# A two-layer transformer block on one core: new instruction order, score masks on GpSimd, three buffers of exponentials, paired products

## The chip, the cores and the metric

The kernel runs on one core of a Trainium2 chip. The metric is device microseconds from launch to end, the median of several runs. The core has five engines with a queue each: TensorE (PE, matmuls), VectorE (DVE), ScalarE (ACT), GpSimd (POOL) and SyncE (SP), which here only issues DMAs. Each queue runs in order, and queues meet only at semaphores. POOL can't read PSUM, where PE writes.

## The reference, cut to what matters

Eight sequences (batches) of 512 tokens with 256 features pass through two layers. Sixteen heads have 16 features each, T = 512, D = 256.

```python
# layer 0 (causal)
xm = layernorm(x) * (1 + sc_a) + sh_a
q, k, v = split(xm @ Wqkv)
scores = where(causal, q @ k.T * hd ** -0.5, -inf)
x = x + gt_a * ((softmax(scores) @ v) @ Wproj + bproj)
xm = layernorm(x) * (1 + sc_m) + sh_m
x = x + gt_m * (gelu(xm @ W1 + b1) @ W2 + b2)
# layer 1 (no mask)
h = sln(x, w)                      # layernorm, then gamma(w) * . + beta(w)
out = (softmax(q @ k.T) / 16) @ v  # q, k, v of h
h1 = out @ Wp.T + bp + x
return sln(h1, w) + h1
```

Scores, exponentials and sums must be as accurate as float32.

## The kernel before, in words

Batches follow each other as in a pipeline. Everything that an engine does is cut into named pieces, and one written-out list of names sets the order for all engines at once: each engine walks the list and does its own part of each name (`run_passes`, `one_pass`). Pass i of the list RING works on layer 0 of batch i, on layer 1 of batch i-1 and on the close of batch i-2. There are passes -1 to 9. Pass -1 has a list of its own (FIRST), and in passes 0, 8 and 9 the same RING is walked and the names of batches that don't exist are skipped. The names:

- `s`, a scan: one matmul of bf16 cuts of q and k for one head and 128 queries (L808) into one of two banks SX; in layer 0 a second small matmul (L811) adds -3e38 above the diagonal. DVE reduces the bank to the negated row maxima MX (L625). 64 scans for each layer of a batch: in layer 0 they are 128, 256, 384 or 512 columns wide, in layer 1 always 512.
- `nm..` and `max..`: POOL cuts the maxima of eight heads into three bf16 parts (L440 to L446), PE transposes them (L924), ACT copies them (L551) and issues a DMA that puts them as three more rows beside q (L553). The two halves of a layer are `a` and `b`.
- `a` and `p`: one step of attention, for four heads and 128 keys. PE makes four transposed score tiles (L795), three at `a` and one at `p`, and in layer 0 adds the mask CAUSAL_T to each with a second matmul (L798). ACT takes the exponentials into E (L502), which has two buffers. At `p` PE also forms the product of the step before with V (`pv`, L783), four heads side by side in 32 columns of the array each, in float32, so that each head has two instructions. 16 steps for a layer of a batch. At each fourth step ACT copies the sum OP out to OE (L489).
- `pack`, `recip`, `scale`, `proj`: SP moves the row sums (L338) and outputs (L340) by DMA, DVE inverts the sums (L743), they go through DRAM and come back spread out (L346, L351), DVE scales (L746), PE projects (L865) and DVE adds and takes statistics (L724 to L637). POOL takes the power -0.5 (L420).
- `q`, `k`, `v`, `turn`, `up_n`, `down_n`: the dense matmuls (L890, L865, L878, L911) through two banks DN. `stackq`, `stackk`: six DMAs each that put the three bf16 cuts of q or k into QS or KS (L386).
- `norm_o` and `close1`: the last norm. DVE writes (x - mean) * rstd into OUT (L672), POOL multiplies by gamma (L465), adds beta to the residual (L467) and adds both (L470), and SP stores (L374).

ACT fills the buffer of E for step n only when the product of step n-2 is done:

```python
wait(act, pv_done, at["step"].at(1, -1))          # L500
```

## Time and profile before

| | us |
|---|---|
| median of 3 runs (lowest to highest) | 1468.91 (1466.01 to 1469.76) |
| the profiled execution's own time | 1477.51 |
| its span, first to last instruction | 1475.7 |
| busy: PE, DVE, ACT, POOL | 1288.3, 866.4, 676.6, 230.4 |
| TensorE clock granted, mean | 0.925 of full speed |

The busy time of PE counts each matmul until its modelled end, and ends overlap with the next start. What a matmul takes from the stream is the distance from its start to the next start. A slice of the profile page is a fortieth of the span, 36.9 us, and its digits are tenths.

### The profile page before, as it was taken

Reading aid. Unit: us, or ns where it says so; the run is one execution under the profiler, and the core shown is the slowest. Engines: PE = TensorE matmul, PEld = TensorE weight load, DVE = VectorE, ACT = ScalarE, POOL = GpSimd, SP = SyncE. Lnnn points to the kernel's source line nnn. Section 1 sums busy time; section 2 is a strip of 40 time slices with the busy share of each in tenths; the row PEclk is TensorE's granted clock in tenths of the full one; section 3 lists DMA queues with packets and bytes.
Section 4 is the critical chain, followed back from the end, with each engine's and each line's share of the span. In section 5 each row is a group of like instructions: output and inputs, shape, how many; then the busy total and the mean of one; then the engine's idle time right before and its main releaser. Section 6 shows DMA issues by size and latency. Waiting matters only on the chain.

```text
span 1475.7 us, 19136 instructions
## 1 busy us (share of the span) xinstructions
PE 1288.3 (87%) x7052; PEld 614.3 (42%) x7052; DVE 866.4 (59%) x1739; ACT 676.6 (46%) x1328; POOL 230.4 (16%) x256
## 2 busy tenths in 40 slices
PE   6795979999889998999899989999899988995871
PEld 5343534444434543454444544354444542442211
DVE  2633367755876468746875487747775576425611
ACT  1061116465446445545556544545546545650360
POOL 3003000210112002300222003200221020202002
PEclk8597979999989999999999999999999999996685
DMA  6305030411514041501532061503341142014002
GB/s 171 113 16 130 1 84 18 106 27 16 124 32 114 2 104 51 131 1 21 134 78 55 4 136 28 118 2 70 84 103 30 16 117 53 2 16 122 1 1 52
DMA packets 57924, 91.61 MB, mean 62 GB/s; under 512 B 10622, under 2 KB 21470, under 8 KB 57830
## 3 DMA queue, kind: packets, MB, share of 16 engines
q1 hardware_dynamic: 56822, 89.57, 26.3%
q8 instruction: 56, 0.92, 0.3%
q10 hardware_dynamic: 1008, 0.81, 0.2%
q14 instruction: 38, 0.31, 0.1%
HBM read 25.46 MB, written 4.77 MB: 20 GB/s over the span
## 4 chain that ended last, share of the span: by engine, by line
PE 62%; DVE 17%; issue 6%; DMA 5%; ACT 4%; SPq 3%; POOL 1%; ACTq 0%; POOLq 0%; DVEq 0%
PE SX L808 11%; PE OP L783 11%; PE DN L865 10%; PE SC L795 10%; DVE MX L625 8%; PE DN L911 7%; PE DN L890 7%; DMA KS<-PART 2%; DMA OC<-OE 2%; DVE STAT L632 2%; ACT E L502 2%; SPq L386 2%; PE SX L811 2%; PE DN L878 1%; PE SC L798 1%
## 5 line engine op out<-in xcount | busy, mean ns | idle before, releaser
L625 DVE TENSOR_REDUCE MX<-SX 128x1 f32<-128x512 f32 (+3 forms) x1024 | 557.5, 585 | 297.4 <-PE SX L811 192.3
L502 ACT ACTIVATE E<-SC 128x512 f32<-128x512 f32 (+3 forms) x1024 | 469.6, 521 | 384.3 <-PE SC L795 194.1
L808 PE MATMUL SX<-KS,QS 96*128 96x512 bf16 (+3 forms) x1024 | 334.3, 370 | 81.9 <-DVE MX L625 70.4
L795 PE MATMUL SC<-QS,KS 99*128 99x512 bf16 (+3 forms) x1024 | 302.8, 356 | 20.1 <-ACT E L502 9.6
L783 PE MATMUL OP<-E,V 128*32 128x512 f32 (+3 forms) x2048 | 241.3, 544 | 1.1 <-ACT E L502 1.1
L795 PEld LDWEIGHTS SC<-QS,KS 99*128 99x128 bf16 x1024 | 98.7, 100 | 295.0 <-ACT E L502 181.4
L808 PEld LDWEIGHTS SX<-KS,QS 96*128 96x128 bf16 x1024 | 101.0, 101 | 228.3 <-DVE MX L625 159.9
L911 PE MATMUL DN<-XT,W 128*128 128x512 f32 x256 | 123.0, 606 | 2.7 <-ACT HID L544 1.8
L890 PE MATMUL DN<-XT,WQKV 128*128 128x512 f32 x256 | 119.4, 610 | 2.4 <-DVE X L686 1.3
L420 POOL TENSOR_TENSOR RSTD<-VE,HALF 128x4 f32<-128x4 f32 x32 | 32.5, 1017 | 545.5 <-DVE VE L637 545.5
L865 PE MATMUL DN<-W,HID 128*128 128x256 f32 x512 | 117.2, 382 | 0.0
L811 PE MATMUL SX<-CAUSAL,ID 128*128 128x128 bf16 x512 | 109.7, 233 | 0.0
L798 PE MATMUL SC<-CAUSAL_T,ID 128*128 128x128 bf16 x512 | 108.3, 227 | 0.0
L865 PEld LDWEIGHTS DN<-W,HID 128*128 128x128 f32 x512 | 95.1, 190 | 12.7
L865 PE MATMUL DN<-WP,OC 128*128 128x256 f32 x256 | 65.9, 415 | 34.0 <-DVE OC L746 23.9
L890 PEld LDWEIGHTS DN<-XT,WQKV 128*128 128x128 f32 x256 | 48.4, 195 | 56.9 <-issue 47.7
L865 PEld LDWEIGHTS DN<-WP,OC 128*128 128x128 f32 x256 | 52.4, 210 | 46.5 <-DVE OC L746 26.3
L783 PEld LDWEIGHTS OP<-E,V 128*32 128x32 f32 x2048 | 41.2, 110 | 69.0 <-issue 41.8
L724 DVE TENSOR_TENSOR TMP<-DN,ROW 128x512 f32<-128x512 f32 x32 | 22.0, 689 | 79.3 <-PE DN L865 77.5
L551 ACT ACTIVATE NT<-DN 24x512 bf16<-24x512 bf16 x32 | 18.8, 586 | 108.7 <-PE DN L924 102.0
L544 ACT ACTIVATE HID<-DN,VF 128x512 f32<-128x512 f32 x64 | 44.0, 687 | 51.2 <-PE DN L911 50.7
L525 ACT ACTIVATE XT<-DN,FM 128x512 f32<-128x512 f32 x48 | 35.2, 783 | 68.2 <-PE DN L878 68.2
(89 smaller groups left out, 984.2 us busy)
## 6 DMA issues: line engine op xcount, KB each, us to landing
QS<-PART SPq DMA_DIRECT2D x96, 256.0 KB, 5.3
KS<-PART SPq DMA_DIRECT2D x96, 256.0 KB, 7.6
OC<-OE SPq DMA_DIRECT2D x64, 128.0 KB
RB<-recip_sums SPq DMA_DIRECT2D x64, 128.0 KB, 2.6
XIN<-in_x SPq DMA_DIRECT2D x8, 512.0 KB, 9.5
ROW<-row_vectors SPq DMA_DIRECT2D x8, 512.0 KB, 3.8
out<-OUT SPq DMA_DIRECT2D x8, 512.0 KB, 2.9
W<-in_w SPq DMA_DIRECT2D x2, 1024.0 KB, 7.2
```

Of the source, the lines that this page charges most:

```text
L502: a.activation(E[:, at["step"].index() % 2, j, lo:T], SC[(4 * s + j) % 3][:, lo:T], ACT.Exp, scale=HD ** -0.5 if attend == 0 else 1.0)\
L525: a.activation(XT[:, ft, :], bank(ft)[:], ACT.Identity, scale=FM[:, first * KT + ft, bass.ds(b, 1)], bias=FM[:, (first + 1) * KT + ft, bas ...
L544: a.activation(HID[:, ht, :], bank(0)[:], ACT.Gelu, bias=B1[:, ht:ht + 1])\
L625: v.reduce_max(MX[:, qt, h:h + 1], SX[at["scan"].index() % 2][:, 0:w], AX.X, negate=True)\
L783: ins = t_.matmul(OP[32 * j:32 * j + 32, lo:T], V[attend][:, kt, h * VW:h * VW + 32], E[:, (at["step"].index() - 1) % 2, j, lo:T], start=k ...
L795: ins = t_.matmul(SC[u % 3][:, lo:T], KS[attend][0:ALL_ROWS, h, kt * P:kt * P + P], QS[attend][0:ALL_ROWS, h, lo:T], start=True, stop=atte ...
L798: ins = t_.matmul(SC[u % 3][:, lo:lo + P], ID16[:], CAUSAL_T[:], start=False, stop=True)
L808: ins = t_.matmul(bank[:, 0:w], QS[layer][0:CUT_ROWS, h, qt * P:qt * P + P], KS[layer][0:CUT_ROWS, h, 0:w], start=True, stop=layer == 1)
L811: ins = t_.matmul(bank[:, qt * P:w], ID16[:], CAUSAL[:], start=False, stop=True)
L865: ins = t_.matmul(psum[:, t % 2 * D:t % 2 * D + D], rows[:, kt, t * P:t * P + P], weights(kt), start=kt == 0, stop=kt == depth - 1)
L890: ins = t_.matmul(psum[:], WQKV[n][:, kt, lo:lo + P], XT[:, kt, :], start=kt == 0, stop=kt == KT - 1)
L911: ins = t_.matmul(psum[:], W1[:, kt, ht * P:ht * P + P], XT[:, kt, :], start=kt == 0, stop=kt == KT - 1)
```

## The change

The 11 passes are now written as three lists without skipped names: HEAD (passes -1, 0 and 1 together), RING (each of the passes 2 to 6) and TAIL (passes 7, 8 and 9 together). RING has 128 `s`, 32 `a`, 32 `p`, 16 `o` and 8 `t`; HEAD has 233 `s` and 48 steps, TAIL 151 `s` and 48 steps.

- The mask matmul of the scores (L798) is gone. POOL sets the entries of E above the diagonal to zero after the exponentials, one `affine_select` for each step of layer 0 over the 128 columns of four heads (128 in all). PE waits for it before the product.
- E has three buffers. The product is a name of its own, `o`, and does two steps at once (two times eight instructions). The copy of OP is `t`.
- For batch 0 of layer 0 and batch 7 of layer 1 the maxima go by four heads (`nm0_0`, `max0_0`, ...) and not by eight.
- `proj1`: POOL adds beta to the residual into RH. `gain1`: DVE forms (x - mean) * gamma, `close1`: DVE multiplies by rstd and adds RH. The three POOL operations go. The last batch is stored in two halves.
- The row sums have a semaphore of their own, so that the reciprocal doesn't wait for the four DMAs of the outputs; for the last batch ACT issues these four. `recip` and the loading of row vectors are parted (`row0`, `row1`). `keep0`'s copy on DVE goes: POOL reads XIN.
- The low cuts of q0 and k0 of batch 0 are made by DVE.

```diff
+HEAD = """
+    stat_a norm_a turn_a q0 mods stackq0 k0 stackk0 rows s s s s s s s s s s s s s s s s s s nm0_0 s s max0_0 s s
+    v0 s s s s s a row0 p s s s a s keep0 s p nm0_1 s s s s a s max0_1 s s s s p s s s s o s a s s s p a o s p a t
+    nm0_2 s s s p a max0_2 p s o a p s s a s s p stat_a a o p s s s norm_a t a s p a s o s nm0_3 turn_a p max0_3
+    q0 a p o a p a t p o a p o t pack0 k0 recip0 scale0 proj0 stackq0 v0 norm_m turn_m stackk0 s s up_0 s s up_1 s
+    s s s up_2 s s s s up_3 s s s s s s s s s up_4 s s up_5 s up_6 s s s s up_7 s s s s down_0 s s s s down_1 s s
+    nm0a max0a down_2 s s down_3 s a s row0 s s norm_1 keep0 p a s s turn_1 s s s s q1 p s stackq1 stat_a o s k1 s
...
 RING = """
+    row0 o s s a stackq1 p s s a stackk1 t s p s s s s s s o s s a pack1 s s p s a row1 s p s s s a s s p s s nm0b
+    s s recip1 o s s a s s p s s s max0b t s s s s a s scale1 p s a s o s s p a s o s p s a s p s t proj1 s a s p
+    a o p a s p s s s o keep0 gain1 s t a s p s a o nm1a close1 s p s stat_a a max1a s v1 p s a o norm_a s t p s
+    turn_a pack0 s a s s recip0 q0 s p s a o s stackq0 s p a scale0 s s p k0 a s s proj0 s s norm_m p v0 a o s p s
+    t turn_m a s s o p s s a s up_0 s p stackk0 s up_1 s up_2 s s nm1b o s s up_3 s hold1 s up_4 s s max1b s s
+    up_5 s s up_6 s s up_7 s s a s down_0 p s s a s down_1 s t p s down_2 s a s s p down_3 a o s p s a s p s s
+    norm_1 o s s t a s s turn_1 s nm0a s s p s max0a a s o p s s a s q1 s p k1""".split()
+TAIL = """
...
+    o p a p t q1 a o p a p k1 stackq1 stackk1 o s s s s t s s s s s s s s s s s s nm1_0 s s
+    s s max1_0 s s v1 s s a s s s p pack1 s a s s s p s nm1_1 a s o p s s a s s max1_1 p s s s s s recip1 o s s a
...
-        E = sb("E", [P, 2, 4, T])
+        E = sb("E", [P, 3, 4, T])
...
+                if kind == "attend":
+                    s, layer, half = what
+                    if half and layer == 0:
+                        lo = P * (s % TT)
+                        block = E[:, at["tick"].index() % 3, :, lo:lo + P]
+                        wait(pool, exp_done, at["head"].at(1, 4))
+                        g.affine_select(out=block, in_=block, compare_op=ALU.is_ge, fill=zero, base=0,
+                                        pattern=[[0, 4], [1, P]], channel_multiplier=-1)\
+                            .then_inc(masked_pool, 1)
...
-                            wait(act, pv_done, at["step"].at(1, -1))
+                            wait(act, pv_done, at["tick"].at(1, -2))
...
+            def product(at, layer, s, n):
+                wait(pe, exp_done, at["step"].at(4, 4 * n + 4))
+                if layer == 0:
+                    wait(pe, masked_pool, at["masked"].at(1, n + 1))
...
-                if attend == 0:
-                    ins = t_.matmul(SC[u % 3][:, lo:lo + P], ID16[:], CAUSAL_T[:], start=False, stop=True)
...
+                    if what == "proj1":
+                        wait(pool, row1_dma, at["rows1"].at(16))
+                        wait(pool, dense_done, at["dense"].at(1, 2))
+                        g.tensor_tensor(RH[:], TMP[:], ROW1[:, 1:2, :].to_broadcast([P, TT, D]), ALU.add)\
+                            .then_inc(plus_pool, 1)
...
+                elif what == "gain1":
+                        v.scalar_tensor_tensor(OUT[:, t, :], TMP[:, t, :], MV[:, t, 0:1], ROW1[:, 0, :],
+                                               ALU.subtract, ALU.mult).then_inc(gain_dve, 1)
+                elif what == "close1":
+                        v.scalar_tensor_tensor(OUT[:, t, :], OUT[:, t, :], RSTD[:, t:t + 1], RH[:, t, :],
+                                               ALU.mult, ALU.add).then_inc(norm_dve, 1)
```

## Rows read from the trace of the kernel before

**Rows 1.** Stretches: us; busy (count) of PE, PEld, DVE, ACT, POOL; clock; DMA; GB/s.
```profile
0.00:220.80 220.80, 166.35 (x816) 92.37 (x816) 96.10 (x222) 50.53 (x104) 28.50 (x42) 0.82 0.33 86
...
376.70:1189.00 812.30, 760.28 (x4363) 367.96 (x4362) 538.94 (x1076) 424.37 (x831) 140.82 (x150) 0.98 0.29 65
1189.00:1475.70 286.70, 213.61 (x1028) 83.30 (x1026) 130.77 (x245) 117.15 (x229) 40.99 (x38) 0.83 0.20 46
```
**Rows 2.** The same for the two parts of one middle pass.
```profile
540.40:620.00 79.60, 72.62 (x471) 33.76 (x469) 61.17 (x115) 41.04 (x96) 19.53 (x18) 0.98 0.48 112
620.00:701.30 81.30, 77.91 (x404) 39.69 (x404) 46.13 (x102) 43.70 (x72) 8.59 (x12) 1.00 0.11 21
```
**Rows 3.** Timeline of PE in a middle pass: start, us, instruction.
```profile
641.94 1.93 PE L911 MATMUL DN<-XT,W 128*128 128x512 f32 x4
643.71 0.38 PE L808 MATMUL SX<-KS,QS 96*128 96x512 bf16 x1
...
646.64 0.22 PE L811 MATMUL SX<-CAUSAL,ID 128*128 128x128 bf16 x1
646.79 1.07 PE L783 MATMUL OP<-E,V 128*32 128x512 f32 x8
647.79 0.39 PE L795 MATMUL SC<-QS,KS 99*128 99x512 bf16 x1
...
648.35 0.22 PE L811 MATMUL SX<-CAUSAL,ID 128*128 128x128 bf16 x1
648.41 0.43 PE L865 MATMUL DN<-W,HID 128*128 128x256 f32 x1
```
**Rows 4.** Groups by line on PE and POOL: count, busy, mean ns, idle before.
```profile
L798 PE MATMUL SC<-CAUSAL_T,ID 128*128 128x128 bf16 x512 | 108.3, 227 | 0.0
L403 POOL TENSOR_SCALAR_AFFINE_SELECT ID<-ID 128x128 f32<-128x128 f32 (+1 forms) x2 | 0.5, 292 | 0.2 <-POOL CAUSAL_T L400 0.2
```
**Rows 5.** Groups on DVE: one operation on two SBUF inputs, two lines.
```profile
L728 DVE TENSOR_TENSOR XR<-XR,TMP 128x512 f32<-128x512 f32 x16 | 18.6, 1165 | 0.5
L728 DVE TENSOR_TENSOR R<-XR,TMP 128x512 f32<-128x512 f32 x16 | 11.1, 692 | 0.5
```
**Rows 6.** Chain of waits at the start: start, us, what.
```profile
44.11 1.17 DVE MX L625 x2
...
70.68 2.76 DMA QS<-NT
...
119.56 4.51 DMA OC<-OE
...
148.18 3.61 PE DN L911 x4
```
**Rows 7.** Timeline: first score matmul of batch 1 on PE.
```profile
218.96 0.39 PE L795 MATMUL SC<-QS,KS 99*128 99x512 bf16 x1 [2.22 <-DMA QS<-NT]
```
**Rows 8.** Timeline near the end, DVE, SP, PE and POOL.
```profile
1330.69 1.23 DVE L695 TENSOR_TENSOR PART<-X,PART 128x1024 bf16<-128x1024 f32 x1
...
1337.02 4.51 SPq L386 DMA_DIRECT2D QS<-PART  x6
...
1353.26 1.03 PE L808 MATMUL SX<-KS,QS 96*128 96x512 bf16 x2 [8.39 <-DMA KS<-PART]
...
1377.18 0.22 POOL L440 TENSOR_SCALAR NMP<-MX 128x32 bf16<-128x32 f32 x1 [19.88 <-DVE MX L625]
...
1382.44 1.97 PE L795 MATMUL SC<-QS,KS 99*128 99x512 bf16 x4 [1.42 <-DMA QS<-NT]
```
**Rows 9.** Timeline of the last 36 us, the lines of the close.
```profile
1439.90 1.96 SPq L340 DMA_DIRECT2D OC<-OE  x2
1444.99 0.55 DVE L743 RECIPROCAL RR<-RS 128x64 f32<-128x64 f32 x1 [35.60 <-DMA OC<-OE]
...
1464.82 2.34 POOL L465 TENSOR_TENSOR OUT<-OUT,ROW 128x1024 f32<-128x1024 f32 x1 [1.50 <-DVE OUT L672]
...
1471.89 0.39 SPq L374 DMA_DIRECT2D out<-OUT  x1
```

More of the change, by code:

```diff
@@ L78 @@
 ADDS = {"proj0": {"dense": 2, "res": 2}, "proj1": {"dense": 2}, "down_0": {}, "down_2": {},
         "down_1": {"dense": 1, "res": 1}, "down_3": {"dense": 1, "res": 1},
-        "hold1": {"hold": 1}, "recip0": {"sums": 1, "rows0": 1, "bias": 1},
-        "recip1": {"sums": 1, "rows1": 1}, "pack0": {"pack": 1}, "pack1": {"pack": 1},
-        "scale0": {"scale": 1}, "scale1": {"scale": 1},
-        "keep0": {"keep": 1, "x_in": 1}, "close1": {"close": 1}, "stat_a": {},
+        "hold1": {"hold": 1}, "row0": {"rows0": 1, "bias": 1}, "row1": {"rows1": 1},
@@ L84 @@
+        "pack0": {"pack": 1}, "pack1": {"pack": 1}, "recip0": {"sums": 1}, "recip1": {"sums": 1}, "scale0": {"scale": 1}, "scale1": {"scale": 1},
+        "gain1": {"gain": 1}, "keep0": {"x_in": 1}, "close1": {"close": 1, "norm": 1}, "stat_a": {},
         "mods": {}, "rows": {}, "stackq0": {}, "stackq1": {}, "stackk0": {"stack0": 1}, "stackk1": {"stack1": 1}}
@@ L97 @@
 COUNTS = ("dense", "res", "bias", "maxima", "max0", "max1", "hold", "pack", "sums", "scale", "rows0",
[L98 to L99 removed]
+          "rows1", "x_in", "gain", "close", "stack0", "stack1", "high", "low", "norm", "head", "tick",
+          "step", "masked", "group", "scan", "halves")
 class Count:
@@ L122, in run_passes @@
     at["x_in"].n = 1
-    for i in range(-1, B + 2):
-        one_pass(at, work, i)
+    one_list(at, work, HEAD, (-1, 0, 1))
+    for i in range(2, B - 1):
+        one_list(at, work, RING, (i,))
+    one_list(at, work, TAIL, (B - 1, B, B + 1))
 def do_chunk(at, work, chunk, b):
@@ L155, in one_pass @@
+            work(at, "attend", (s, layer, 1), b)
+            at["head"].n += 4
+            at["tick"].n += 1
+        elif what == "o":
+            layer, b, s = products.pop(0)
+            products.pop(0)
+            work(at, "product", (s, layer), b)
+            at["step"].n += 2
+            at["masked"].n += 2 * (layer == 0)
+        elif what == "t":
+            layer, b, g = groups.pop(0)
+            work(at, "out", (g, layer), b)
+            at["group"].n += 1
         elif what == "s":
@@ L171, in two_layers @@
+            work(at, "scan", (layer, h, qt), b)
+            at["scan"].n += 1
+        else:
+            do_chunk(at, work, what, chunks[what].pop(0))
+    assert not steps and not products and not groups and not tiles
 def two_layers(nc, x, cond_t, wqkv0, wproj0, w1, w2, wada, wqkv1, wp1, wgb1, vecs, bv1, bp1, out):
@@ L545, in work @@
                         .then_inc(dense_done, 1)
-                elif what in ("max0a", "max0b", "max1a", "max1b"):
-                    n, first = int(what[3]), H // 2 * "ab".index(what[4])
+                elif what == "pack1" and b == B - 1:
+                    wait(act, out_act, at["group"].at())
+                    wait(act, scaled_dve, at["scale"].at())
+                    for j in range(4):
+                        act.dma_start(OC[64 * (j % 2):64 * (j % 2) + 64, j // 2, :],
+                                      OE[32 * j:32 * j + HD, :, :]).then_inc(compact_dma, 16)
+                elif what.startswith("max"):
+                    n, heads = int(what[3]), maxima_heads(what)
+                    rows = 3 * (heads.stop - heads.start)
                     psum = bank(0)
@@ L715, in work @@
                     wait(dve, bias_pool, at["bias"].at())
-                    if what == "proj0":
-                        wait(dve, close_pool, at["close"].at(3))
+                    wait(dve, plus_pool, at["gain"].at())
                     if what == "down_1":
@@ L832, in work @@
                     for j in range(3):
-                        score_t(at, attend, s, j)
+                        score_t(at, layer, s, j)
                     return
-                if kind == "last":
-                    pv(at, what, STEPS - 1)
+                if kind == "product":
+                    s, layer = what
+                    for n in range(2):
+                        product(at, layer, s + n, n)
+                    return
+                if kind != "chunk":
                     return
```

355 lines of the change are left out of this document (189 added, 166 removed), and 5 rows, old and new, of the table BEHIND.

## The prediction, made before the changed kernel ran

> **What bounds the kernel now.** I read the busy time by stretches first, then the order of starts on TensorE, then the chain at both ends. Cut where the attention of batches 2 and 7 begins, the span falls into a start, five full passes of 162.5 us (812.3 / 5) and an end [rows 1]. In the five passes PE is busy 94% at a clock of 0.98; no other engine passes 66%. At the start PE is busy 75% at a clock of 0.82, and in the last 286.7 us also 75% at 0.83. So there are three questions: what leaves PE's stream in the full passes, how much of the idle time at the ends can be filled, and what waits at the ends get shorter.
>
> A full pass has two unlike parts [rows 2]. In the first (scans of layer 1, attention of layer 0, the small dense pieces) PE is busy 72.6 of 79.6 us and DVE 61.2: PE does long dense pieces in which DVE, with only two banks of scans, runs dry, and then waits for DVE in turn. In the second (up, down, attention of layer 1) PE is busy 77.9 of 81.3 us and DVE only 46.1: PE alone is the bound there.
>
> Busy time overstates small matmuls. The masks of the scores stand with 108.3 us, 227 ns each [rows 4], but from a 128-column mask to the next start it is 0.06 us [rows 3]. That is the price that counts where PE is full.
>
> **The change part by part.** The sum is made against the profiled execution: 1477.5 us, 1.8 more than its span.
>
> *Masks of the scores.* 512 leave PE, 64 in each batch: 64 x 0.058 = 3.7 us a pass, all in the first part. In their place POOL has 16 selects of 512 elements a batch. The trace has selects of 128 elements at 0.29 us [rows 4] and POOL operations of 1024 elements with two inputs at 2.34 us [rows 9]. So one costs at least 0.29 and, by four times the small one or half the large one, at most 1.17 us; I take 1.0, nearest to both upper prices. 16 us beside the 19.5 us that POOL has in this part of 79.6 us [rows 2] is well covered. The new wait (product for mask) has queued behind it on PE all that follows. It is hidden because the pair of products comes later in the list than its exponentials, with `s` or an `a` between in nearly all cases, and ACT has a third buffer to write meanwhile. Without that cover each pair would cost 1.0 us: 8 pairs, 8 us a pass.
>
> *Paired products.* The start behind a mask is 0.15 us away when a product follows and 0.06 when a dense matmul does: 0.09 to get in. The two rounds of a product take 2 x 0.44 (four dense instructions of 512 columns take 1.77 us) = 0.89, but the next score comes after 1.00: 0.11 to get out [rows 3]. So a visit to the 32-column form costs 0.2 us besides its work. 16 visits fewer in a pass: 3.1 us, some 10 of 16 in the first part. No products stand back to back in these rows, so it is bounded: 0 to 3.1 us; I take nearly all.
>
> *What the five full passes get.* Up to 6.8 us leaves PE's stream. But 5.6 of it leaves the first part, where DVE keeps 61.2 busy us and its own idle moments behind the dense pieces. RING has the same number of scans ahead of `norm_m` as before (75), so the part's other limit doesn't move. I count the second part's 1.2 us whole and of the first part's 5.6 us two thirds: 5 us a pass, 25 us for five. Ends: 0 (the first part is as long as ever), and 6.8 plus the 7 us in which PE is idle there now, 13.8 a pass.
>
> *The DVE work* changes little: the copy of `keep0` goes, four passes over 256 columns come. It is not what ends a wait. Nothing for that.
>
> *The start.* (a) The first attention waits for 41 scans, which begin at 44.1 and end at 70.7: 0.65 us each [rows 6]. Now 18 scans do, so it begins some 15 us earlier. The end of that attention then hangs on the last of all 64 scans: 44 + 42 = 86, and v0, the maxima's chain and four steps put it near 110, where the copies out lie at 119.6 now: -9. (b) From there to the first up matmul are 28.6 us of waits in series [rows 6]; the sums no longer wait for the outputs' DMAs: -2. (c) From that matmul to the first scores of batch 1 are 70.8 us [rows 6, 7]: up, down, then scans, turn_1, q1 and k1, and only then the maxima. HEAD puts all 41 scans into up and down and the scores right behind down_3. That stretch needs 8 x 1.77 for up, 4 x 3.5 for down (the same columns twice) and 41 x 0.2 for scans = 36.5, some 2 more for waits: -32. (d) q1, k1 and turn_1 now stand under the attention of batch 1: +8 us of PE; with 87 scans in the same stretch DVE holds it up: +6. Pass 1 gets its own -5. Sum for the start: -34 us, ends -15 and -50.
>
> *The end.* (a) Pass 7: -5. (b) The last cuts of k1 are ready at 1331.9, but the DMAs of q and k stand in SP's queue behind `recip1` and start at 1337.0; those of k take from 1341.5 to 1353.3 until scans start. TAIL puts the stacks ahead of `pack1`, so k's can go at 1331.9: 9.6 us earlier at best; I take -8. (c) From the first scan to the last copies out are 86.6 us (1353.3 to 1439.9): 32 scans of 0.75, a chain of 5.3 until scores start, and 16 steps [rows 8, 9]. By groups of four heads the 64 scans run alongside the steps: 64 x 0.75 = 48, v1 and other pieces between them 5, chain 5.3, four steps of 2.5 (four exponentials of 512 columns), product and copy 2: 70. That is -16. (d) The close: the reciprocal comes 5.1 us after the last DMA's issue, -3 with sums apart and ACT issuing the outputs; three POOL operations from 1464.8 to the store at 1471.9 (7.1 us) turn into two halves of DVE work, of which one has to be done before the first store: -6 [rows 9]. In the new `proj1` POOL adds beta (2.34 us) ahead of the power, but the statistics on DVE cover it. Sum for the end: -38 us, ends -22 and -52.
>
> *Three buffers, the split of row0 and recip, DVE's cuts for batch 0:* nothing by themselves; they let the order above hold. SP has no wait that is new in kind, and `row0` stands at the head of RING, where its data has long been due when `proj0` comes. It does stand ahead of the first masks on POOL: where the row vectors land late, the masks are late too. I count this within the 5 us.
>
> **Sum.** -34 - 25 - 38 = -97: 1477.5 - 97 = 1380.5. The median of the runs stands at 1468.91 / 1477.51 = 0.994 of the profiled execution, so 1372 us.
>
> **A rule against the change.** One DVE operation with both inputs in SBUF takes 692 ns on average in one place and 1165 in another [rows 5]; the second place is where POOL works on large tiles. So a busier POOL can slow DVE. The Trainium skill (SBUF — State Buffer, section Who interferes with whom) says that a DVE instruction with two SBUF inputs and a GpSimd instruction that reads SBUF shut each other out for the whole of one of them, and that a reduction is never held up. By that rule, the trace agrees, and scans are safe while `gain1`, `close1`, `scale` and the residual adds are not.
>
> **The rivals.**
>
> 1. *The idle time of the first part is filled as well.* For: PE is no longer the fuller engine there, and DVE is at 61 of 79.6. Against: two banks, and the same dense pieces. 8.8 us more for each of seven passes: 1380.5 - 62 = 1319, or 1311 as a median; anything between counts here down from 1345.
> 2. *DVE sets the pace of the first part.* The passes stay at 162.5 us, and the start and end give only some -50: 1427, or 1419 as a median. For: 75 scans ahead of `norm_m` as before. Against: DVE isn't full in any stretch.
> 3. *Masks hold up DVE.* Some 11 operations with two SBUF inputs a pass, each waiting for one mask of 1.0 us: 11 x 8 = 88 us, 1460. For: the 1165 ns [rows 5]. Against: masks cover only a fifth of the part's time, and the three long POOL operations of `close1`, which did the same, go.
> 4. *POOL becomes the bound (slower).* If a select over four blocks takes far more than its element count says, the first part lasts 16 T + 19.5 us instead of 75. It eats the whole gain of 97 / 8 = 12 us a batch from T = 4.2 us on; at T = 4.5 it is 91.5, 17 us a batch more than forecast: 1372 + 135 = 1507. For: nothing in the trace shows this shape. Against: both nearest rows give under 1.2 us.
>
> **How the numbers follow.** Forecast 0.55 (its own range 1345 to 1395), rival 1 0.22, rival 2 0.13, rival 3 0.05, rival 4 0.05. The range 1315 to 1425 takes in rivals 1 and 2 but for their far ends, and is what the ends of the terms give: -50 - 69 - 52 leads to 1299, -15 - 0 - 22 to 1432. About 0.3%, 4 us, is what a measurement can tell from no change. Faster 0.93, same 0.02, slower 0.05 (rival 4).
>
> **What the changed profile would show.** No L798 group; 128 selects on POOL of about 1.0 us (over 4: rival 4). Sixteen product instructions in a row with 0.44 us from round to round across the pair. Full passes of 157 us; 149 speaks for rival 1, 162 for rival 2. First scores near 60 us, first up matmul near 137, scores of batch 1 near 176. At the end, scans of the last layer some 13 us earlier than 1353 less what went before, 70 us from there to the last copies, and no POOL operation behind the power. The DVE mean of residual adds and of `scale` shows rival 3. I am wrong if the full passes don't get shorter though PE's stream did, or if the ends, which carry 72 of the 97 us, wait for something that I don't see in the list, as DMAs queued behind each other on SP.

## The result and the profile after

The changed kernel takes 1389.97 us (median of 4 runs, 1387.18 to 1396.24) where the kernel before takes 1469.34 beside it (1466.01 to 1473.45): a ratio of 0.948, 95% interval 0.945 to 0.951. The forecast was 1372 with a range from 1315 to 1425. The direction held and the range held the time, but the forecast was 18 us too low, and its parts were further off than their sum. The profiled execution took 1391.76 us, 11.3 more than the sum of 1380.5. The rest of the 18 us is the step from a profiled execution to the median, 0.999 here and not 0.994: the one execution of the kernel before that was profiled is 8 us longer than its median, longer than each of its timed runs.

First the stretches, cut as in [rows 1] where the attention of batches 1, 2 and 7 begins. Columns: stretch; its us; busy (count) of PE, PEld, DVE, ACT, POOL; clock; DMA; GB/s. Busy time and clock are those of the changed kernel:

```profile
0.00:186.50 186.50, 135.62 (x703) 74.23 (x703) 81.97 (x193) 46.67 (x99) 32.88 (x59) 0.90 0.31 85
186.50:363.50 177.00, 161.21 (x818) 74.85 (x818) 109.26 (x219) 89.99 (x174) 34.45 (x44) 0.92 0.24 58
363.50:1127.90 764.40, 731.96 (x4040) 355.16 (x4039) 533.84 (x1091) 415.94 (x830) 173.23 (x220) 0.99 0.30 70
1127.90:1390.00 262.10, 207.13 (x999) 85.88 (x997) 141.68 (x267) 117.22 (x232) 37.85 (x55) 0.88 0.21 47
```

| | before | after | difference | forecast |
|---|---|---|---|---|
| start, to the attention of batch 2 | 376.7 | 363.5 | -13.2 | -34 |
| five full passes | 812.3 | 764.4 | -47.9 (-9.6 each) | -25 |
| from batch 7 to the end | 286.7 | 262.1 | -24.6 | -38 |

The five passes gave nearly twice what was forecast, the two ends half of it. Part of the first is the execution and not the kernel: the kernel of experiment 6, which has the median of the kernel before, was profiled at 1466.96 us, with 371.0, 802.9 and 291.2 us in the three stretches. Against it the passes gained 38.5 us and the ends 36.6. The RING of the changed kernel took 764.4 to 769.8 us in four profiles (changed, 7, 8 and 12), so a pass is known to about 1 us, in the kernel before to about 2. In the passes PE is busy 28.3 us less (760.28 to 731.96), 5.7 a pass, and idle 19.6 us less (52.0 to 32.4), 3.9 a pass. The forecast took 6.8 us a pass off PE's stream and let its idle time grow by 1.8.

Two products in a row on PE in a middle pass (start, us, instruction), to be laid beside [rows 3]:

```profile
598.78 1.92 PE L888 MATMUL OP<-E,V 128*32 128x512 f32 x16
600.64 0.39 PE L899 MATMUL SC<-QS,KS 99*128 99x512 bf16 x1
```

From the first of sixteen instructions to the score behind them are 1.86 us; two products apart took 2 x 1.00 [rows 3]. With one entry of 0.09 us saved as well, a pair is worth 0.23 us; the forecast had 0.2.

The groups that answer to [rows 4, 5] (line, form, count; busy, mean ns; idle before, and releaser):

```profile
L505 POOL TENSOR_SCALAR_AFFINE_SELECT E<-E 128x512 f32<-128x512 f32 x128 | 85.4, 669 | 338.6 <-ACT E L585 338.5
...
L833 DVE TENSOR_TENSOR XR<-XR,TMP 128x512 f32<-128x512 f32 x16 | 15.9, 992 | 0.5
```

A select takes 0.67 us, under the 1.0 that was taken, and of PE's waits only one, of 0.6 us, has the select as its releaser. The operation on XR became shorter (1165 to 992 ns) though POOL got busier; the same one into R stays at 692. The selects have no part in it: with the masks back on PE (experiment 1) it takes 990 ns. Nor do the three POOL operations of the old close stand beside it in the middle pass looked at: there the long one lies beside POOL's cut of 2.13 us and ends 0.54 us behind it, in both kernels. In the kernel before it begins 0.76 us after the cut,

```profile
614.61 2.13 POOL L433 TENSOR_TENSOR PART<-X,PART 128x1024 bf16<-128x1024 f32 x1
...
615.37 1.91 DVE L728 TENSOR_TENSOR XR<-XR,TMP 128x512 f32<-128x512 f32 x1
```

and in the changed one 1.02 us after it (588.18 behind 587.16), and so takes 1.65 us.

What lengthens it in other passes was not looked at. DVE's reductions of 512 columns take 685 ns in both kernels. Both facts agree with the rule quoted in the prediction (the Trainium skill, SBUF — State Buffer, section Who interferes with whom).

Where the wait at both ends is (timeline and chain; start, us, instruction), for [rows 6 to 9]:

```profile
63.83 0.81 PE L899 MATMUL SC<-QS,KS 99*128 99x512 bf16 x3
...
113.90 3.24 SPq L404 DMA_DIRECT2D OC<-OE  x4
...
140.48 1.95 PE L1014 MATMUL DN<-XT,W 128*128 128x512 f32 x4 [0.35 <-issue]
...
184.75 0.81 PE L899 MATMUL SC<-QS,KS 99*128 99x512 bf16 x3
...
1272.31 4.38 SPq L464 DMA_DIRECT2D KS<-PART  x6
...
1272.91 1.23 DVE L801 TENSOR_TENSOR PART<-X,PART 128x1024 bf16<-128x1024 f32 x1
...
1284.92 1.04 PE L909 MATMUL SX<-KS,QS 96*128 96x512 bf16 x2 [12.43 <-DMA KS<-PART]
...
1341.63 1.11 POOL L540 TENSOR_SCALAR NMP<-MX 128x16 bf16<-128x16 f32 x1 [13.95 <-DVE MX L723]
...
1361.79 3.58 ACTq L641 DMA_DIRECT2D OC<-OE  x4
```

The copies out are four DMAs at both ends, and the times here are those of the first one's issue. The prediction's rows have a later one of the four (119.56 and 1439.90); the same first issues in the kernel before are

```profile
117.61 3.25 SPq L340 DMA_DIRECT2D OC<-OE  x4
...
1438.61 3.25 SPq L340 DMA_DIRECT2D OC<-OE  x4
```

The reader is to see six distances: first scores at 63.8 (73.5 before), from the copies of the first attention to the first up matmul 26.6 us (30.6 before), from there to the scores of batch 1 44.3 (70.8 before), from the last cut of k to the scans that read it 10.8 (1274.14 to 1284.92; 21.3 before), from these scans to the last copies 76.9 (85.4 before), and from those to the end 28.2 (37.1 before).

### The profile page after: what moved, and what is told of

Read it like the earlier page. It is cut to its first block, busy times and chain, and to the rows that moved or that the text cites. A ratio compares the mean times of both kernels' runs of the same rounds, so it can differ in the third digit from the quotient of the medians.

```text
span 1390.0 us, 18485 instructions
## 1 busy us (share of the span) xinstructions
PE 1235.9 (89%) x6556; PEld 590.1 (42%) x6556; DVE 866.8 (62%) x1767; ACT 669.8 (48%) x1334; POOL 278.4 (20%) x378
## 4 chain that ended last, share of the span: by engine, by line
PE 67%; DVE 13%; ACT 5%; DMA 3%; issue 2%; SPq 2%; POOL 1%; ACTq 0%; DVEq 0%; POOLq 0%
PE DN L968 16%; PE OP L888 11%; PE SX L909 11%; PE SC L899 10%; DVE MX L723 10%; PE DN L1014 8%; PE DN L993 7%; ACT E L585 4%; PE DN L981 2%; PE SX L912 2%; DMA KS<-PART 1%; SPq L464 1%; DMA recip_sums<-RR 1%; DMA RB<-recip_sums 1%; DVE OUT L773 1%
## 5 line engine op out<-in xcount | busy, mean ns | idle before, releaser
L723 DVE TENSOR_REDUCE MX<-SX 128x1 f32<-128x512 f32 (+3 forms) x1024 | 557.1, 586 | 281.2 <-PE SX L912 176.0
L585 ACT ACTIVATE E<-SC 128x512 f32<-128x512 f32 (+3 forms) x1024 | 460.9, 523 | 380.9 <-PE SC L899 303.6
L909 PE MATMUL SX<-KS,QS 96*128 96x512 bf16 (+3 forms) x1024 | 344.0, 361 | 81.1 <-DVE MX L723 54.0
L899 PE MATMUL SC<-QS,KS 99*128 99x512 bf16 (+3 forms) x1024 | 281.2, 348 | 16.6 <-ACT E L585 9.6
L888 PE MATMUL OP<-E,V 128*32 128x512 f32 (+3 forms) x2048 | 215.2, 538 | 3.1 <-DVE X L793 1.4
L505 POOL TENSOR_SCALAR_AFFINE_SELECT E<-E 128x512 f32<-128x512 f32 x128 | 85.4, 669 | 338.6 <-ACT E L585 338.5
L993 PE MATMUL DN<-XT,WQKV 128*128 128x512 f32 x256 | 123.0, 626 | 0.9 <-ACT XT L616 0.9
L912 PE MATMUL SX<-CAUSAL,ID 128*128 128x128 bf16 x512 | 113.0, 227 | 0.0
L888 PEld LDWEIGHTS OP<-E,V 128*32 128x32 f32 x2048 | 54.9, 112 | 110.4 <-issue 83.2
L540 POOL TENSOR_SCALAR NMP<-MX 128x32 bf16<-128x32 f32 (+1 forms) x36 | 8.7, 241 | 278.5 <-DVE MX L723 232.0
L1014 PEld LDWEIGHTS DN<-XT,W 128*128 128x128 f32 x256 | 45.5, 191 | 43.2 <-issue 34.0
```

Of the source, the lines that this page charges most:

```text
L505: g.affine_select(out=block, in_=block, compare_op=ALU.is_ge, fill=zero, base=0, pattern=[[0, 4], [1, P]], channel_multiplier=-1)\
L585: a.activation(E[:, at["tick"].index() % 3, j, lo:T], SC[(at["head"].index() + j) % 3][:, lo:T], ACT.Exp, scale=HD ** -0.5 if layer == 0 e ...
L723: v.reduce_max(MX[:, qt, h:h + 1], SX[at["scan"].index() % 2][:, 0:w], AX.X, negate=True)\
L888: ins = t_.matmul(OP[32 * j:32 * j + 32, lo:T], V[layer][:, kt, h * VW:h * VW + 32], E[:, (at["step"].index() + n) % 3, j, lo:T], start=kt ...
L899: t_.matmul(SC[(at["head"].index() + j) % 3][:, lo:T], KS[layer][0:ALL_ROWS, h, kt * P:kt * P + P], QS[layer][0:ALL_ROWS, h, lo:T], start= ...
L909: ins = t_.matmul(bank[:, 0:w], QS[layer][0:CUT_ROWS, h, qt * P:qt * P + P], KS[layer][0:CUT_ROWS, h, 0:w], start=True, stop=layer == 1)
```

## The experiments

Each kernel was timed against the kernel before on the same chip, which took 1464 to 1467 us beside them. Ten of them start from the changed kernel (1390 us); of these 3 and 10 differ from it in the order of the middle passes alone, 5, 9 and 11 in the masks or pairs as well. 4 and 6 start from the kernel before. "Full passes" are the five stretches of the profiled execution, by five.

**1. Masks back on PE** (the changed kernel otherwise).

```diff
-                t_.matmul(SC[...][:, lo:T], KS[...], QS[...], start=True, stop=True).then_inc(head_full, 1)
+                ins = t_.matmul(SC[...][:, lo:T], KS[...], QS[...], start=True, stop=layer == 1)
+                if layer == 0:
+                    ins = t_.matmul(SC[...][:, lo:lo + P], ID16[:], CAUSAL_T[:], start=False, stop=True)
+                ins.then_inc(head_full, 1)
```

POOL's select and PE's wait for it are left out.

> The changed kernel, its order and the rest as they are, but the mask of the scores is again the second matmul on PE and POOL has no select. Theory A (PE's stream is what a full pass costs): 64 masks of 0.058 us come back in each of 8 batches, 3.7 us a pass, full passes 156.6 instead of 152.9 us, in all +30 us, 1420. Rival B (the new order made the passes shorter, and what left PE's stream in the first part is hidden behind DVE): +0 to +8 us, full passes 153 to 154.

Measured: 1391.17 us (ratio 0.949, 0.946 to 0.952), full passes of 153.3 us. Moving the masks is worth nothing that can be measured in this order. The forecast had counted it with 3.7 us of PE's stream a pass.

**2. No pairs.** The second product of a pair goes behind the next scan or score; where a dense piece comes next, the two stay together.

```diff
-                    for n in range(2):
-                        product(at, layer, s + n, n)
+                    product(at, layer, s, 0)
+                    late.append((kept, layer, s + 1, 1))   # issued behind the next s, a or p
```

> The changed kernel, but the second product of each pair is put behind the next scan or group of scores on PE (before a dense piece it stays behind the first). Theory A: a pair saves 0.2 us for one visit less to the 32-column form and, by the starts in the trace of after (409 instead of 433 ns from round to round inside a pair), some 0.1 more; 128 pairs x 0.33 = +42 us less those that stay paired, 1425 to 1432, full passes 157 to 158. Rival B: the passes have slack for it, +0 to +12 us.

Measured: 1417.07 us (0.967, 0.964 to 0.971), full passes of 157.1 us. Pairs are worth 4.2 us a pass, 27 us in all.

**3. The old order of the middle passes, first try.** RING has the names in the order of before, with all new mechanisms (pairs, three buffers, masks on POOL, the new close); the ends stay as changed.

> The changed kernel with RING in the order of the kernel before (products where they stood, now in twos at each second p; recip1, scale1 and close1 moved by a few names so that nothing waits in a new place); HEAD and TAIL as changed. Five full passes run in the old order with the new mechanisms. Theory A: masks 3.7 and pairs 5.3 us a pass are most of the 9.6 us that a full pass lost, so full passes take 153 to 155 us and the whole 1390 to 1402. Rival B: the order is most of it, full passes 158 to 161 us and the whole 1415 to 1430.

Measured: 1480.98 us (1.011, 1.007 to 1.014), passes of 169.9. Slower than the kernel before, though every part that was added is in it.

**4. Masks on POOL in the kernel before**, nothing else changed.

```diff
+                if kind == "attend" and half and layer == 0:
+                    wait(pool, exp_done, at["head"].at(1, 4))
+                    g.affine_select(out=block, in_=block, compare_op=ALU.is_ge, fill=zero, ...)
-                    ins = t_.matmul(SC[u % 3][:, lo:lo + P], ID16[:], CAUSAL_T[:], start=False, stop=True)
```

> The kernel before with one edit: the mask of the scores leaves PE and is a select on POOL, two buffers and single products as they were. Theory A: 3.7 us a batch, -30 us, 1440, if the select (0.67 us in the trace of after) is over when the product comes. Rival B: no gain, since the first part is held by DVE: 1465 to 1470. Rival C: without pairs and a third buffer PE stands behind the select, up to 0.7 us in 128 steps: 1470 to 1530.

Measured: 1564.79 us (1.068, 1.063 to 1.072), passes of 175.5. Over the five passes PE waits 21 times, 47.5 us in all, for a select that came last. The timelines of POOL and PE show the longest such place of one pass:

```profile
591.77 2.35 POOL L478 TENSOR_TENSOR OUT<-OUT,ROW 128x1024 f32<-128x1024 f32 x1
594.08 2.48 POOL L480 TENSOR_TENSOR TMP<-TMP,ROW 128x1024 f32<-128x1024 f32 x1
596.64 2.34 POOL L483 TENSOR_TENSOR OUT<-OUT,TMP 128x1024 f32<-128x1024 f32 x1
598.93 0.69 POOL L424 TENSOR_SCALAR_AFFINE_SELECT E<-E 128x512 f32<-128x512 f32 x1
```

```profile
599.76 0.87 PE L798 MATMUL OP<-E,V 128*32 128x384 f32 x4 [3.65 <-POOL E L424]
```

A select stands in POOL's queue behind the three operations of the old `close1`, and PE stands for 3.65 us. Three more stalls of this pass come when a select stands behind the power (0.39 and 2.35 us) or behind a cut (2.44 us). The clock follows. It has two levels, 1.0 (2.4 GHz) and 0.5 (1.2 GHz), and a stretch shows their mean: 0.91 over the five passes. Around two of these stalls, the one of 2.35 us before 585.48 and the one of 3.65 us before 599.76:

```profile
584.00:586.00 2.00, 0.52 (x8) 0.23 (x8) 0.83 (x2) 0.00 (x0) 1.33 (x2) 0.65 0.00 0
586.00:594.00 8.00, 8.00 (x39) 2.21 (x31) 4.52 (x8) 4.21 (x9) 3.46 (x3) 0.50 0.00 1
...
596.00:598.00 2.00, 0.11 (x1) 0.00 (x0) 2.00 (x2) 0.82 (x3) 1.92 (x2) 1.00 0.00 0
...
600.00:610.00 10.00, 9.90 (x45) 3.07 (x38) 6.07 (x10) 4.40 (x12) 1.91 (x3) 0.50 0.15 51
...
612.00:614.00 2.00, 2.00 (x15) 0.55 (x13) 1.29 (x2) 1.08 (x3) 0.00 (x0) 1.00 0.04 8
```

Behind the first stall PE works without a gap at 0.50 for 8 us, is back at 1.00 when the next stall begins, and works 10 us more at 0.50 behind that one: each stall is paid a second time.

**5. As 3, with masks on PE.**

> As e3_old_ring, but with the masks of the scores on PE as well: RING in the old order, products in twos, three buffers, new closing norm, no work of attention on POOL. So far: masks back on PE cost nothing (full passes 153.3), unpairing costs 4.2 us a pass, and the old order with all the new mechanisms takes 169.9 us a pass, more than the 162.5 of before. Theory C: the masks on POOL are what the old order can't bear (their select stands behind other work on POOL and bare before the product), and pairs give their 4 us there too: full passes 157 to 160 us, 1415 to 1430, and the rest of the way to 153 is the order. Rival D: my old order with new names has waits of its own (recip1, row vectors), whatever the masks do: full passes 167 to 171 us, 1470 to 1480.

Measured: 1488.33 us (1.014, 1.010 to 1.020), passes of 170.6. Its trace shows a fault of the order that experiments 3 and 5 walk. The copies of layer 1 (`pack1`) come only at the head of the next pass, and `scale1` soon behind them, so that DVE reaches the scaling before the inverted sums are back:

```profile
535.83 0.54 DVE L853 RECIPROCAL RR<-RS 128x64 f32<-128x64 f32 x1
536.39 0.33 SPq L411 DMA_DIRECT2D recip_sums<-RR  x1
...
545.51 1.23 DVE L857 TENSOR_TENSOR OC<-OC,RB 128x1024 f32<-128x1024 f32 x1 [5.00 <-DMA RB<-recip_sums]
```

DVE stands there 24.7 us in the five passes, 4.9 a pass, and the scans with it; in experiment 9 this wait is gone. So 3 and 5 say little on the old order itself; experiments 9 to 11 repeat them without that fault. Against each other they still show what the masks do there: on POOL (169.9) they cost nothing against PE (170.6), though PE stands 12.3 us ahead of its products in 3 and not at all in 5.

**6. Three buffers of exponentials in the kernel before.**

```diff
-        E = sb("E", [P, 2, 4, T])
+        E = sb("E", [P, 3, 4, T])
-                            wait(act, pv_done, at["step"].at(1, -1))
+                            wait(act, pv_done, at["step"].at(1, -2))
...
```

To make room two small tensors of the setup (MF and GF) lie inside OUT here.

> The kernel before with a third buffer of exponentials and nothing else: ScalarE may be a step further ahead. The score banks (three) still hold it, and the product still goes one step behind. Theory: no change, 1458 to 1470, because no row of the trace of before shows ScalarE waiting for a product. Rival: the third buffer is what smooths the passes, 2 to 5 us each, 1430 to 1450.

Measured: 1466.12 us (1.000, 0.998 to 1.002), passes of 160.6. Nothing by itself, as forecast.

**7. The start: scans of batch 1 put off.** Of the 40 scans of batch 1 that HEAD has ahead of `down_3`, 26 go behind it (the expectation says 30 of 41).

> The changed kernel with 30 of the 41 scans of batch 1 that HEAD puts into up and down of batch 0 moved behind down_3, where PE waits for the norm, so that q1 and k1 of batch 0 and their stacks come sooner; the first scores of batch 1 come later for it. Theory: what paces pass 1 is the chain to k1's stack and the 64 full scans of layer 1 behind it, not the first scores: batch 2 starts 4 to 8 us earlier than at 363.5, 1382 to 1386. Rival: the attention of batch 1 paces it, batch 2 starts 0 to 10 us later, 1390 to 1400.

Measured: 1412.73 us (0.963, 0.960 to 0.966). The scores of batch 1 come 33 us later, those of batch 2 25 us. My theory fell: of the 33 us pass 1 gives back only 8, so the attention of batch 1 has to begin early.

**8. Maxima by eight heads at both ends.**

```diff
-    return (layer, b) in ((0, 0), (1, B - 1))       # grouped()
+    return False
```

with `nm0_0` to `nm0_3` and `nm1_0` to `nm1_3` put together by two where the last head of each is scanned, and the steps that read them held back.

> The changed kernel with the maxima by eight heads for batch 0 of layer 0 and batch 7 of layer 1 too; steps and products that then lack their maxima are held back to the next max. Theory: at the end attention starts 12 us later (16 more scans of 0.7 us) and its last eight steps stand behind the last scan instead of four, 10 us more; at the start the same with shorter scans, some 5 us: 1402 to 1410. Rival: the scans themselves set the end (55 us for 64), and steps by ScalarE catch up: 1390 to 1397.

Measured: 1440.47 us (0.983, 0.980 to 0.987), full passes of 154.0, but the attention of batch 2 begins at 391.4 (363.5) and the stretch from batch 7 takes 285.0 (262.1). Maxima by four heads carry 50 us of this order: 28 at the start, 23 at the end, which is more than the 38 us that both ends gained in all. Without them this order of the start is slower than the kernel before (391.4 against 376.7).

**9. The old order rebuilt, masks on PE.** Row vectors and reciprocal at the head of the pass, the last products of layer 1 inside the same pass, `close1` in its old place. HEAD and TAIL follow at their seams.

```diff
 RING = """
-    row0 o s s a stackq1 p s s a stackk1 t s p s s s s s s o s s a pack1 s s p s a row1 s p s s s a s s p s s nm0b
+    recip1 row1 row0 s s v1 s s s s a s s stackq1 s s p s stackk1 s scale1 a s s keep0 p s a o p s s proj1 s a
...
```

> The changed kernel with its middle passes in the order of the kernel before, rebuilt without the faults of e3 and e5 (row vectors and reciprocals asked for at the start of the pass, the last two steps of layer 1 inside the same pass, stored output and close in their old places), with pairs, three buffers and the fused norm, and with the masks as TensorE matmuls. The two ends stay as changed. A full pass took 162.5 us before, 152.9 in the changed kernel, and without pairs 157.1. Theory (the order itself carries about half of the gain of a pass): 162.5 - 4.2 for the pairs = 158 us a pass, the time near 1390 + 5 x 5 = 1415 us. Rival (pairs and the cheaper close carry it and the order is worth nothing): 153 to 154 a pass, the time near 1392. Second rival (e3's and e5's slow passes were no artefact, pairs and this order don't go together): 168 or more a pass, near 1470.

Measured: 1465.58 us (0.999, 0.997 to 1.001), passes of 167.2. The second rival (168 or more a pass, near 1470) came closest: this order and pairs don't go together. With pairs it is 4.7 us a pass slower than the kernel before, although it has every part of the change in the middle passes but the order and the masks.

**10. As 9, with masks on POOL.**

> As e5c_old_order_masks_on_pe, with the masks as selects on GpSimd. The difference between the two is what the selects cost where the order leaves no room for them. In the new order it was 0 (1390 against 1391 us). Theory: in the old order a select (0.67 us) stands between the exponentials and the product pair of most steps, and behind GpSimd's closing work in some, as in e4 where a pass grew by 13 us: 6 to 13 us a pass more than e5c, 30 to 65 us in all. Rival (the third buffer of exponentials gives the selects their cover whatever the order): within 2 us a pass of e5c, within 10 us in all.

Measured: 1494.47 us (1.020, 1.017 to 1.022), passes of 172.4. The selects cost 5.2 us a pass there, a little under the theory, against nothing in the new order. Over the five passes PE now stands 17.8 us ahead of its products (0.0 in 9), and 17.0 of it in five places, one in each pass:

```profile
548.33 0.38 SPq L426 DMA_DIRECT2D ROW<-row_vectors  x1
...
554.14 2.34 POOL L554 TENSOR_TENSOR XR<-XIN,ROW 128x1024 f32<-128x1024 f32 x1 [28.56 <-DMA ROW<-row_vectors]
556.43 1.23 POOL L507 TENSOR_SCALAR_AFFINE_SELECT E<-E 128x512 f32<-128x512 f32 x2
...
557.17 3.21 PE L890 MATMUL OP<-E,V 128*32 128x512 f32 x16 [3.88 <-issue]
```

The load of layer 0's row vectors stands behind the sums in SP's queue, as in the kernel before. POOL's add to the residual waits for it, two selects wait behind the add, and the products behind these (the view puts PE's wait down to issue, but the first of the two selects ends at 557.1). The prediction named this risk: "It does stand ahead of the first masks on POOL: where the row vectors land late, the masks are late too." The changed kernel loads these vectors earlier, and POOL waits for them 0.9 us in the whole run. By these rows 17 of the 26 us that the selects cost here hang on one load, which the changed kernel asks for early because `row0` and `recip` are parted. That is a reading: a kernel with the old order and an early `row0` was not run.

**11. As 9, with the products one by one.**

```diff
-            at["step"].n += 2
+            at["step"].n += 1                       # "q" before each odd p, "o" for the second
```

> The kernel of e5c_old_order_masks_on_pe (middle passes in the old order, masks as TensorE matmuls, three buffers, fused norm) with the products one by one in the middle passes, each where the kernel before has it; what is left of the difference to the kernel before is the third buffer, the closing work and the places of the row loads. e5c took 167.2 us a pass, the kernel before 162.5, and the kernel before with three buffers 160.6. Theory (pairs don't pay in the old order: two of them together hold back the scans and scores behind them, so that VectorE and ScalarE wait): 161 to 163 a pass, the time 25 us under e5c, near 1441 us. Rival (pairs pay 4 us a pass everywhere, as in the new order, and the new closing work with its places costs the old order 9): 171 a pass, near 1485 us.

Measured: 1442.01 us (0.983, 0.980 to 0.987), passes of 162.5, as the theory had it. In the old order pairs cost 4.7 us a pass; in the new one they bring 4.2. (HEAD and TAIL keep their pairs here.)

**12. K's stacks issued by ScalarE at both ends.**

```diff
+                elif what in ("stackk0", "stackk1") and (int(what[-1]), b) in ((0, 0), (1, B - 1)):
+                    ...
+                                act.dma_start(KS[n][r:CUT_ROWS:CUTS, :, :], PART[:, 1, part, :, :])
```

> The changed kernel; K's six stacking DMAs of the first batch of layer 0 and of the last batch of layer 1 are issued by ScalarE and no longer by SyncE, behind Q's. In the trace SyncE issues Q's from 1268.25 for 4.0 us and K's from 1272.31 for 4.4 us, K's parts were all cut by 1274.1, and the first scan that reads them starts at 1285.6. Theory (the issuing of twelve DMAs one behind another is on the path at both ends): the scans start 2 to 3 us earlier at each end, the time 1385 to 1387 us. Rival (the last part of K is cut late enough that one queue issues it in time, and the landing takes what it takes): nothing, 1390 within 1 us.

Measured: 1392.81 us (0.949, 0.947 to 0.952), nothing. The two queues in the trace of this kernel, to be laid beside 1272.91 and 1284.92 above:

```profile
1271.61 5.28 ACTq L643 DMA_DIRECT2D KS<-PART  x6
...
1273.12 1.23 DVE L813 TENSOR_TENSOR PART<-X,PART 128x1024 bf16<-128x1024 f32 x1
...
1284.25 1.03 PE L921 MATMUL SX<-KS,QS 96*128 96x512 bf16 x2 [11.55 <-DMA KS<-PART]
```

The last cut of k is ready at 1274.35, and in either kernel the last of K's six DMAs are issued behind it. From there to the scans are 9.9 us, 10.8 in the changed kernel: 0.9 us, lost among the runs. The rival was right. No kernel of these beats the changed one.

## Why: point by point

**The five full passes.** All of them in one table, from the same view (812.3 / 5 and so on), with PE's busy and idle time a pass:

| full pass | us | PE busy | PE idle | clock |
|---|---|---|---|---|
| before | 162.5 | 152.1 | 10.4 | 0.98 |
| before, three buffers (6) | 160.6 | 150.3 | 10.3 | 0.99 |
| before, masks on POOL (4) | 175.5 | 157.9 | 17.6 | 0.91 |
| old order, singles, masks on PE (11) | 162.5 | 150.7 | 11.7 | 0.97 |
| old order, pairs, masks on PE (9) | 167.2 | 151.1 | 16.1 | 0.97 |
| old order, pairs, masks on POOL (10) | 172.4 | 152.3 | 20.1 | 0.94 |
| new order, singles, masks on POOL (2) | 157.1 | 150.4 | 6.8 | 0.98 |
| new order, pairs, masks on PE (1) | 153.3 | 147.8 | 5.5 | 1.00 |
| changed: new order, pairs, masks on POOL | 152.9 | 146.4 | 6.5 | 0.99 |

The rows that four of the lines rest on (11, 9, 2 and 1; the changed kernel's stands above):

```profile
373.10:1185.40 812.30, 753.67 (x4335) 365.74 (x4334) 532.69 (x1081) 425.03 (x830) 119.74 (x141) 0.97 0.31 68
```

```profile
369.80:1205.80 836.00, 755.68 (x4335) 377.85 (x4334) 532.19 (x1081) 420.41 (x831) 119.72 (x141) 0.97 0.30 66
```

```profile
373.00:1158.60 785.60, 751.85 (x4040) 349.85 (x4039) 536.42 (x1091) 414.87 (x831) 174.09 (x220) 0.98 0.29 68
```

```profile
363.40:1129.90 766.50, 739.23 (x4360) 375.05 (x4359) 534.13 (x1091) 416.07 (x830) 119.16 (x140) 1.00 0.30 69
```

*The order is the step that failed.* The prediction said that the first part's other limit doesn't move, because RING has as many scans ahead of `norm_m`, and cut the gain to 5 us. Experiments 9 and 1 differ in the order of the middle passes and its seams alone (pairs, masks on PE, three buffers and the new close in both): 167.2 and 153.3 us a pass, with 16.1 and 5.5 us of PE's idle time. So do 10 and the changed kernel, with masks on POOL: 172.4 and 152.9. With single products (11 and 2, which also differ in the masks) it is 162.5 and 157.1 us, 11.7 and 6.8 idle. The count of 75 scans is right, but it starts at the head of the list, and the lists start in different places of the pass: the old one has 6 scans ahead of the first `a`, the new one 2, and up to the first up there are 81 and 82. So from the pass's first scores to its first up matmul there are 75 scans before and 80 now. `v1` moved too: it stood ahead of the first `a` and is now in the first half, which so has 32 `v` matmuls for 16. These are PE's scans and its `v` matmuls in the two halves of one pass, of before (540.4:627.7, then 627.7:701.3):

```profile
L808 PE MATMUL SX<-KS,QS 96*128 96x512 bf16 (+1 forms) x75 | 25.0, 375 | 6.5 <-DVE MX L625 6.3
...
L808 PE MATMUL SX<-KS,QS 96*128 96x512 bf16 (+3 forms) x54 | 14.2, 310 | 1.3 <-DVE MX L625 1.3
...
L865 PE MATMUL DN<-WQKV,XT 128*128 128x256 f32 x16 | 3.7, 386 | 0.2 <-DVE X L686 0.2
```

and of the changed kernel (515.1:602.2, then 602.2:667.9):

```profile
L909 PE MATMUL SX<-KS,QS 96*128 96x512 bf16 (+1 forms) x80 | 28.3, 376 | 4.6 <-DVE MX L723 4.3
...
L968 PE MATMUL DN<-WQKV,XT 128*128 128x256 f32 x32 | 7.2, 379 | 0.0
...
L909 PE MATMUL SX<-KS,QS 96*128 96x512 bf16 (+3 forms) x49 | 13.8, 310 | 0.6 <-DVE MX L723 0.5
```

The first half is as long as ever (87.3 and 87.1 us) but holds five scans and the 16 matmuls of `v1` more and less waiting for DVE; the second, without them, falls from 73.6 to 65.7. Rival 1 (idle time of the first part filled) was thus half true: 152.9 us lies halfway between its 149 and the forecast's 157. That the order does it is shown; which single shift in the list (the scans, `v1` or another) was not tried.

*Pairs* were right in price (0.23 us each where 0.2 was taken) and don't stand as a term of their own: whether PE gets to keep them hangs on the order. PE's groups over the five passes, singles (11) and then pairs (9) in the old order:

```profile
L894 PE MATMUL OP<-E,V 128*32 128x512 f32 (+3 forms) x1280 | 149.1, 539 | 0.0
L919 PE MATMUL SX<-KS,QS 96*128 96x512 bf16 (+1 forms) x635 | 193.8, 351 | 41.1 <-DVE MX L731 35.1 <-DMA KS<-PART 5.0
L905 PE MATMUL SC<-QS,KS 99*128 99x512 bf16 (+3 forms) x641 | 189.0, 355 | 13.3 <-DMA QS<-NT 9.6 <-ACT E L593 2.6
```

```profile
L892 PE MATMUL OP<-E,V 128*32 128x512 f32 (+3 forms) x1280 | 132.4, 533 | 0.0
L917 PE MATMUL SX<-KS,QS 96*128 96x512 bf16 (+1 forms) x635 | 198.8, 355 | 55.3 <-DVE MX L729 50.4 <-DMA KS<-PART 3.0
L903 PE MATMUL SC<-QS,KS 99*128 99x512 bf16 (+3 forms) x641 | 193.6, 356 | 21.1 <-DMA QS<-NT 9.8 <-ACT E L591 8.4
```

The products take 16.7 us less in the five passes, but 22.0 are lost in front of scans (14.2 more) and scores (7.8 more). For 1.9 us PE gives DVE no scan and ACT no score, and with only two banks of scans DVE runs dry and PE waits for it in turn. That reading is from the waits; the loss itself is shown by 9 against 11. In the new order the same two lines are 149.7 (2) and 132.1 us (changed), and the idle time ahead of scans goes from 22.2 to 25.2 and ahead of scores from 11.4 to 7.0: there the saving stays.

*Masks*: the step "64 x 0.058 = 3.7 us a pass" failed. With masks on PE a pass has 1.5 us more of busy time and 1.0 less of idle (1 against the changed kernel; the clock is 1.00 for 0.99): the slot that they leave seems to fall into the part in which PE waits anyway, which is argued and not shown. The cover that the prediction named for the selects holds in the new order. Where it is gone they cost 5.2 us a pass (10 against 9, by its rows most of it at the late row vectors) or 13 (4 against before, or 15 against 6), and in the order of 3 and 5 nothing. "Without that cover 8 us a pass" was of the right size, but the price is that of POOL's queue and not 1.0 us for each pair.

**The start** (-13.2 for -34). (a) -3.7 for -9, first issue against first issue: the first scores come 9.7 us earlier (15 forecast), but the last of the 64 scans starts at 96.1, where the sum had 86, and the copies come at 113.9, not 110. (b) -4.0 for -2. (c) From the first up matmul to batch 1's scores 44.3 us where 36.5 + 2 were forecast: -26.5 for -32. (d) failed: pass 1 is 21 us longer and not 9 (184.75 to 363.5 = 178.8, before 218.96 to 376.7 = 157.7). PE is busy 161.2 us in it, 13.1 more than before, and idle 15.8, 8 more. The dense matmuls that were moved in are there (48 of the form 512 columns against 32), 9.9 us for the 8 that were taken. The rest is waiting for DVE and a lower clock: PE's idle time ahead of scans is 12.1 us (5.5 before), and the clock was 0.84 and 0.83 in these two stretches of it, where before pass 1 ran at 0.97:

```profile
186.50:230.00 43.50, 35.80 (x175) 16.67 (x175) 31.64 (x68) 16.79 (x39) 9.79 (x14) 0.84 0.40 98
230.00:270.00 40.00, 34.99 (x196) 11.55 (x196) 27.55 (x47) 22.00 (x51) 8.90 (x14) 0.83 0.11 16
```

The term for DVE was 6 us and there was none for the clock. Experiment 7 shows that putting fewer scans ahead doesn't mend it.

**The end** (-24.6 for -38). (a) From batch 7's attention to the last cut of k 146.2 us where 142.9 were needed before: +3.3 for -5; TAIL has an order of its own for it, and it is no shorter than the old one; why was not looked into. (b) -10.6 for -8. (c) -8.5 for -16: the scans take 56.7 us (1284.92 to 1341.63) and not 53, and from the last maxima to the last copies are 20.2, where chain, four steps, product and copy were put at 17. (d) -8.9 for -9, the POOL operations gone as forecast.

**The rivals.** 1 was half true. 2 (passes stay at 162.5, the ends bring the rest) is what kernel 11 does: 162.5 a pass and 1442 us, so 23 us less than before from the ends, where the rival had 50. The new order took its ground away. 3 fell with the XR operation, which no select lengthens (992 ns with them, 990 without), 4 with the 669 ns of a select. As single changes, however, masks on POOL make the kernel 6.8% slower.

So the forecast came within 11 us of the profiled execution because two larger errors stood against each other: the passes were counted 23 us too long and the two ends 34 us too short. In a pass the stream gave 5.7 us where 6.8 were forecast, and the idle time fell by 3.9 where it was to grow by 1.8. Against the profile of experiment 6 the two errors are 14 and 35 us. That the kernel would get faster by tens of us was argued; that the time came out so near is luck.

## What to carry to other kernels

Work taken off a full engine is worth its stream time only if the order of the list puts the hole where that engine has no waits; measure order and savings crosswise before adding them up, because one saving here had either sign. In a hand-written order count each engine's work between two points of the pass that mean the same in both kernels (here the first scores and the first up matmul), not from the head of the list to a name. Work given to a helper engine waits for whatever stands ahead of it in that engine's queue, here an add that waited for a load. At the two ends of a pipeline look at the granularity of what the first and last stage wait for (maxima by four heads), and price the granted clock along with the idle time.

## What the runs showed of the hardware

- Two products of four 32-column groups in a row take 1.86 us (changed, 598.78 to 600.64), not 2 x 1.00 [rows 3]: the second adds 0.86, which is two rounds of 0.43.
- A select on POOL over 128 x 512 float32 takes 0.64 us on average (4) to 0.67 (changed), where one over 128 x 128 takes 0.29 [rows 4]: less than four times as much.
- TensorE's granted clock fell from 1.0 to 0.5 behind stalls of 2.35 and 3.65 us, and each time stayed there for 8 to 10 us and more in which PE worked without a gap (4, 584 to 612 us). Over the first part of that pass (558.1 to 634.7) the mean was 0.75; the first part of a pass of the kernel before has 0.98 [rows 2]. A pass that got 7.2 us more idle time became 13 us longer, though the masks had left PE's stream.
- DVE's operation on two SBUF inputs (XR) takes 692 ns at best, and 1.91 us (before) and 1.65 us (changed) where it lies beside POOL's cut of 2.13 us, ending 0.54 us behind it. The selects on POOL leave its mean as it is (992 ns with them, 990 without).
